# One-hots of the tensor-product phase: six of eight tiles on ScalarE and two on VectorE, in place of five and three

## The reference, cut to what matters

```python
x_j = node_features[col]                                     # 100000 x 16
m = einsum('ei,ej,ijh->eh', x_j, edge_attr, W_msg_tp) * norm # 100000 x 16
m = silu(m)
m = m @ W_msg_lin * norm_lin
agg = segment_sum(m, row, num_segments=n_nodes)              # 3125 x 16
u = silu(einsum('ni,nh,ihk->nk', node_features, agg, W_upd_tp) * norm_upd)
return node_features + u @ W_upd_lin * norm_lin
```

## Time and profile before

| | |
|---|---|
| median of three runs | 4458.6 us |
| the profiled execution's own time | 4503.67 us |
| its span, first to last instruction | 4501.9 us |
| TensorE matmuls busy | 4343.3 us, 96% |
| VectorE busy | 4111.1 us, 91% |
| ScalarE busy | 3228.1 us, 72% |
| GpSimd busy | 3306.9 us, 73% |
| mean granted TensorE clock, share of full speed | 0.989 |

### The profile page before, as it was taken

One profiled execution on the slowest core, in us unless ns is written; L12 is line 12 of the kernel. 1 busy time (PEld: TensorE's weight loads), 2 busy tenths in 40 slices (PEclk: granted clock), 3 DMA queues, 4 the chain that ended last, 5 costly groups with the idle time before them and its releaser, 6 DMA issues.

```text
span 4501.9 us, 107823 instructions
## 1 busy us (share of the span) xinstructions
PE 4343.3 (96%) x30591; PEld 3227.3 (72%) x30591; DVE 4111.1 (91%) x11847; ACT 3228.1 (72%) x5358; POOL 3306.9 (73%) x2516
## 2 busy tenths in 40 slices
PE   7999999999998999999999999999999998899998
PEld 4767777777775677777767777776777776666666
DVE  7999999999997999999979999997999998888888
ACT  5777777777774777777757777776777776677776
POOL 6788888888884788888847676775676775777776
PEclk8999999999999999999999999999999999999999
DMA  2111111111112322222211111111111111111111
GB/s 59 27 17 18 18 18 17 18 17 18 17 18 55 80 63 63 62 63 62 62 40 27 26 28 27 27 25 42 26 28 27 27 27 25 28 30 30 30 31 25
DMA packets 339795, 152.11 MB, mean 34 GB/s; under 512 B 250726, under 2 KB 325394, under 8 KB 339754
## 3 DMA queue, kind: packets, MB, share of 16 engines
q0 software_dynamic: 104000, 59.31, 10.3%
q1 hardware_dynamic: 235754, 92.30, 8.1%
HBM read 138.66 MB, written 10.00 MB: 33 GB/s over the span
## 4 chain that ended last, share of the span: by engine, by line
PE 66%; DVE 19%; issue 10%; DMA 1%; ACT 1%; DVEq 1%; POOL 1%; another core or an unknown queue 0%; SPq 0%; POOLq 0%; ACTq 0%
PE acc L665 30%; PE rows_ps L838 12%; PE rows_ps L760 7%; PE bank L760 6%; DVE stationary L1330 4%; PE bank L853 3%; DVE one_hot L1302 3%; DVE rows_ps L1424 3%; PE eaT_ps L845 2%; PE rows_ps L748 2%; DVE fields_all L1543 2%; PE rows_ps L669 1%; PE eaT_ps L736 1%; DVE raw L1354 1%; DVE fields_all L1545 1%
## 5 line engine op out<-in xcount | busy, mean ns | idle before, releaser
L665 PE MATMUL acc<-one_hot,stationary 125*128 125x392 bf16 x12000 | 2337.0, 329 | 57.8 <-DVE stationary L1330 33.3
L649 POOL DMA_INDIRECT gathered<-table_l,row_numbers x1200 | 1605.2, 1338 | 452.8 <-issue 333.4
L665 PEld LDWEIGHTS acc<-one_hot,stationary 125*128 125x128 bf16 x12000 | 1147.3, 99 | 734.1 <-DVE stationary L1330 49.9
L956 ACT ACTIVATE distances<-count_hi,fields 125x392 bf16<-125x392 f16 (+1 forms) x2500 | 1222.4, 557 | 0.0
L1330 DVE TENSOR_TENSOR stationary<-mask,parts 125x1024 bf16<-125x1024 bf16 x1500 | 943.6, 683 | 0.2 <-issue 0.2
L941 ACT CAST mask<-is_lo 125x1024 bf16<-125x1024 f32 x500 | 521.7, 1043 | 488.8 <-issue 292.0
L649 POOL DMA_INDIRECT fields_all<-table_l,row_numbers x500 | 673.8, 1348 | 217.6 <-issue 143.2
L1302 DVE TENSOR_SCALAR one_hot<-count_hi,fields 125x392 bf16<-125x392 f16 x2300 | 751.3, 348 | 13.6 <-issue 13.5
L1424 DVE COPY_PREDICATED rows_ps<-near_bits_now,rows_ps 125x320 f32<-125x320 int8 (+3 forms) x1600 | 581.9, 364 | 191.6 <-PE rows_ps L838 121.3
L649 POOL DMA_INDIRECT gathered<-table_l2a,row_numbers x400 | 511.1, 1278 | 265.4 <-DVE parts L1312 122.8
L649 POOL DMA_INDIRECT gathered<-table_l2b,row_numbers x400 | 510.8, 1277 | 244.2 <-DVE parts L1312 121.4
(11 more groups left out here) (221 smaller groups left out, 4807.5 us busy)
## 6 DMA issues: line engine op xcount, KB each, us to landing
near_key<-near_keys_by_chunk SPq DMA_DIRECT2D x300, 122.1 KB
gathered<-table_l,row_numbers POOLq DMA_INDIRECT x1200
fields<-edge_fields SPq DMA_DIRECT2D x500, 31.2 KB
near_key<-near_keys_by_chunk SPq DMA_DIRECT2D x100, 91.6 KB
fields_all<-table_l,row_numbers POOLq DMA_INDIRECT x500
gathered<-table_l2a,row_numbers POOLq DMA_INDIRECT x400
gathered<-table_l2b,row_numbers POOLq DMA_INDIRECT x400
ea<-in_edge_attr SPq DMA_DIRECT2D x100, 62.5 KB
```

What stands on the lines that cost most here:

```text
L649: pool.indirect_dma_start(out=gathered[ph][:, s, t, :], in_=table[ph], out_offset=None, in_offset=bass.IndirectOffsetOnAxis(ap=row_numbers ...
L665: mm = pe.matmul(acc[:, :], stationary[:, s, k, t, :, :].rearrange("p a b -> p (a b)"), one_hot[:, s, t, :], start=first and t == 0 and k ...
L956: ins = act.activation(distances[:, i * n:(i + 1) * n], count_hi[:, 0:n], ACT.Abs, scale=-1.0, bias=fields[:, s, k, t:t + 1].bitcast(F32))
```

## The change

One number is changed, the count of `l1`:

```diff
-        SCALAR_TILES = {"l0": 0, "l1": 5, "l2a": 4, "l2b": 4, "l3": 4}
+        SCALAR_TILES = {"l0": 0, "l1": 6, "l2a": 4, "l2b": 4, "l3": 4}
```

## The result

The changed kernel takes 4470.91 us (median of 11 runs, 4464.03 to 4476.43), the kernel before 4458.60 in the same comparison (11 runs, 4456.81 to 4463.81). The ratio is 1.0025, with a 95% interval of 1.0017 to 1.0032: **12.3 us slower**. The forecast was 4459.6 us, in a range up to 4466; the time lies above it. The profiled execution of after took 4469.29 us with a span of 4467.5.

What follows compares the result with a forecast made beforehand. VectorE's own instruction row, with a round trip to ScalarE (raw, SiLU, split), was taken to set 8.34 us a chunk. 0 (VectorE) + 0.3 (head) + 0.2 (first stretch) + 0.5 (tail) = +1.0 us: 4459.6 us, range 4453 to 4466.

Steps and rivals of the forecast that it cites:

- The period of `l1`: In the changed tensor-product phase, a chunk still takes 8.34 us.
- 0.34 us from raw to split: On VectorE in `l1`: the split still starts 0.34 us after raw messages end, because it waits for the SiLU.
- VectorE's removed comparison at 0: In `l1`, removing VectorE's third one-hot gains 0 per chunk, as the wait for the SiLU covers it.
- The added distance covered by the wait before the copy: On ScalarE in `l1`: the added distance costs 0.50 us, covered by a 1.24 us wait, leaving 0.74.
- The room before the SiLU: On ScalarE in `l1`: 0.64 us idle before the far SiLU, of which 0.31 is left after the 0.33 us delay.
- The combined one-hot: On ScalarE in `l1`: covering six tiles instead of five takes 0.325 us more, 2.25 us in all.
- VectorE's busy time: In `l1`, VectorE's busy time falls by some 35 us with no gain.
- Head, first stretch and tail: First chunk, early chunks and last chunk of `l1`: 0.3, 0.2 and 0.5 us of added time.
- Memory, other phases, DMA queues: Outside the changed phase: a larger distances buffer read as before, nothing issued more or less on SP or POOL; no time added.
- VectorE's work counts in full: Faster rival in `l1`: the split starts 0.24 us sooner, TensorE capping the gain; middle 11 us, 4447.6 us; chance 0.05.
- The added distance isn't covered: Slower rival on ScalarE in `l1`: SiLU 0.19 us later in each of 100 chunks, +19 us, 4477.6 us; chance 0.08.
- The small drift: First stretch of `l1`: ten chunks more or fewer at 8.7 instead of 8.34 us, 4 us, inside the range.

Runs made afterwards that it cites:

- e4: The changed kernel with two distances ahead of the SiLU and four behind it; ratio to the kernel before 1.0041.
- e12: The changed kernel, with VectorE still making a third comparison per chunk in `l1`, into a tile nobody reads; ratio to the kernel before 1.0002.
- e11: The kernel before with 120 tiny VectorE memsets between the tensor-product phase and the next; 4472.61 us in one run.
- e13: The changed kernel; in `l3`, every second chunk's last near-choice copy on VectorE covers seven rows where one is used; ratio to the kernel before 1.0005.

## Why the prediction was wrong

**What held.** *The period of `l1`*: a chunk still takes 8.34 us, and the split still follows the SiLU. The prediction never set VectorE's row against GpSimd's, which has no pause there either; e4 speaks for VectorE's, as said above. The prediction's 0.34 us from raw to split is 0.33 (1823.60 + 0.24 to 1824.17). *VectorE's removed comparison at 0*: right, by e12. *The added distance covered by the wait before the copy*: 0.74 us was to be left, 0.77 was. *The room before the SiLU*: 0.31 forecast, 0.31 measured, and e4 showed what happens beyond it and that the whole room is 0.74 and not 0.64. *The combined one-hot*: 2.25 forecast, 2.256 measured. *VectorE's busy time*: it fell by 24.3 us in 596, so some 34 in the phase, without gain. *Head, first stretch and tail*, summed to +1.0: the phase came out at 828.9 us against 830.0. Unchanged kernels give 828.5 to 830.0, so these small terms are neither borne out nor refuted.

**What failed is one step: "Memory, other phases, DMA queues".** It reads "Nothing is issued more or less on SP or POOL", which is true, and it put the other four phases at exactly 0, with no bound. The term was about +12 us (12.3 by the periods, 12.9 by the length of `l3`), and it covers the miss of 11.3 us. The sentence counts what the change issues; it doesn't ask what of the untouched phases hangs on when things meet. The prediction's own trace had signs of it. In `l3` most of GpSimd's gaps were already those of an issue alone, but not all; its gaps there from 3900 to 4400 us hold these:

```profile
POOL gathered L649 <- DVE parts L1321: 24.2, 18, 2.3
```

Pairs of chunks took anything from 12.06 to 15.38 us in that one execution, so `l3` was sensitive to timing with the program unchanged. And the prediction had itself noted that L1403 is stretched in the first stretch of `l1` (0.400 us against 0.314). It gave no cause; in that trace each L1403 over 0.35 us there ends 0.06 us behind a gather. It didn't carry this to the other phases. Even so only the sensitivity could have been forecast, at one stretched gather more or less per pair, some 0.1 to 0.5 x 49 = 5 to 25 us; that the return would change, and with which sign, no row of before told.

**The rivals.** *VectorE's work counts in full*: refuted, at 8.34 us. *The added distance isn't covered*: its sign came true and its mechanism didn't; the wait before the copy has 0.77 us left and no chunk of `l1` is longer. *The small drift*: within its 4 us.

**What stays open.** Why one execution of before had no steady period in `l3`, with the return at 0.309, isn't known: the place of the code isn't all that decides the pattern. Why the return takes 0.167 us at places -8 and +120 and 0.309 at -4, 0 and +56 isn't shown; the runs show only that it follows the place of the code, and by e11 not with one period for all loops. The Trainium skill ("Advanced Engine Details and Errata", Control Flow Timing) has one figure for a compare-and-branch, about 0.108 us; VectorE's returns here are 0.137 to 0.309, which take in the start of the next instruction. Why the steady pattern with 0.167 is the one with three stretched gathers follows from no formula here; e13 shows that it is a matter of VectorE's phase.

## What to carry to other kernels

Look at every phase, not at the changed one alone, and count an engine's issue gaps as its work: GpSimd was at 81% busy in `l3` and had no pause. But a row without a pause needn't be the bound where two engines hold each other up. Where indirect DMAs run back to back beside VectorE, a shift of 0.15 us can cost 2% of a phase or give it back, so a difference of a few tenths of a per cent between two kernels can come from where the code stands; before it is put down to the edit, give the program its old length with idle instructions and compare again. And when a test of a delay shows nothing, see in its trace that the delay arrived.

## What the runs showed of the hardware that I had not expected

- A loop return on VectorE takes 0.167 or 0.309 us for the same loop, by where its code stands (eight instructions made the difference); on ScalarE 0.160 or 0.231.
- A gather that starts while VectorE multiplies two operands from SBUF is longer by the rest of that instruction less 0.12 us: 0.52, 0.28, 0.15 or 0.12 us on 1.21. A fast comparison or cast on VectorE that starts in about the last 0.65 us of a gather is held to its end (0.65 us for a cast of 0.23).
- More work on VectorE (0.4 us in every second chunk) made a phase 9.4 us shorter.
